# Attention probabilities turned by VectorE and 13 DMAs in place of TensorE, the value product one batch late, GpSimd scaling 13 of 16 batches

## What is computed

```python
scores = jnp.einsum('bhqd,bhkd->bhqk', q, k) / jnp.sqrt(jnp.asarray(HD, x.dtype))
scores = scores + causal_bias
attn = jax.nn.softmax(scores, axis=-1)
out = jnp.einsum('bhqk,bhkd->bhqd', attn, v)
out = out.transpose(0, 2, 1, 3).reshape(b, s, NH * HD)
return out @ wo
```

## Time and profile before

| what | value |
|---|---|
| median of 3 runs | 1897.14 us (1891.51 to 1898.26) |
| profiled execution, first to last instruction | 1893.5 us |
| TensorE busy | 97% |
| VectorE busy | 68% |
| ScalarE busy | 50% |
| GpSimd busy | 29% |
| DMA traffic | 212.37 MB, mean 112 GB/s |

### The profile page before, as it was taken

How to read it: one execution, slowest core, us unless ns; L and a number is a source line. 1 busy time by engine, 2 the same in 40 slices (tenths; PEclk the granted TensorE clock), 3 DMA queues, 4 the chain that set the end, 5 groups by cost and what they waited for, 6 DMA issues and landing times.

```text
span 1893.5 us, 36659 instructions
## 1 busy us (share of the span) xinstructions
PE 1842.4 (97%) x10612; PEld 1359.5 (72%) x10613; DVE 1281.0 (68%) x3173; ACT 949.9 (50%) x3625; POOL 543.2 (29%) x721
## 2 busy tenths in 40 slices
PE   7999999999999999999999999999999999999995
PEld 5887888766668888756667888766667888866663
DVE  4677778754467888764467888764466888855456
ACT  4647776622226777732225777642224777642221
POOL 4752113430022332540032332531031332520014
PEclk9999999999999999999999999999999999999998
DMA  6423220255653330245663340236663331136666
GB/s 165 130 71 107 101 101 6 85 139 143 154 149 102 116 115 7 85 122 142 145 157 89 118 130 27 85 94 147 145 164 93 128 116 44 43 92 149 147 163 172
DMA packets 255292, 212.37 MB, mean 112 GB/s; under 512 B 145826, under 2 KB 226420, under 8 KB 255028
## 3 DMA queue, kind: packets, MB, share of 16 engines
q1 hardware_dynamic: 240808, 174.74, 33.8%
q0 software_dynamic: 13952, 35.33, 6.3%
q10 hardware_dynamic: 380, 0.38, 0.1%
HBM read 137.32 MB, written 73.05 MB: 111 GB/s over the span
## 4 chain that ended last, share of the span: by engine, by line
PE 71%; DVE 9%; ACT 8%; issue 4%; POOL 4%; DMA 3%; SPq 1%; POOLq 0%; DVEq 0%; ACTq 0%
PE ps L930 24%; PE ps L956 12%; ACT parena L1273 8%; PE ps L816 7%; PE ps L896 6%; PE ps L872 4%; PE ps L846 3%; PE ps L861 3%; PE ps L824 3%; POOL qk L591 2%; DVE rope L1601 2%; PE ps L798 2%; PE ps L924 2%; DVE rmax L1621 2%; DVE rope L1605 2%
## 5 line engine op out<-in xcount | busy, mean ns | idle before, releaser
L930 PE MATMUL ps<-arena,xeT 128*128 x1120 | 509.5, 593 | 0.0
L1273 ACT ACTIVATE parena<-ps,nmax 112x112 f32<-112x112 f32 x1024 | 345.6, 387 | 95.3 <-DVE nmax L1622 95.3
L930 PEld LDWEIGHTS ps<-arena,xeT 128*128 128x128 f32 x1120 | 210.1, 190 | 193.5 <-issue 187.3
L591 POOL TENSOR_TENSOR qk<-qk,rope 128x448 f32<-128x448 f32 x128 | 146.3, 1143 | 548.9 <-DVE rope L1605 548.7
L1322 ACT ACTIVATE parena<-ps,er 128x512 f32<-128x512 f32 x140 | 96.2, 687 | 377.1 <-PE ps L930 377.1
L816 PE MATMUL ps<-xnT,wqk_s 128*128 128x224 f32 x1280 | 273.5, 357 | 0.0
L570 POOL DMA_INDIRECT y_in<-sorted_y,pos x114 | 111.2, 975 | 500.6 <-DMA sorted_y<-tarena 397.0
L1273 ACT ACTIVATION_READ_ACCUMULATOR parena<-ps,nmax 112x1 f32 x1024 | 245.9, 240 | 0.0
L896 PE MATMUL ps<-wo_s,oT 128*112 128x256 f32 x1024 | 237.9, 385 | 1.4 <-issue 1.4
L816 PEld LDWEIGHTS ps<-xnT,wqk_s 128*128 128x128 f32 x1280 | 233.5, 191 | 3.1
L1898 DVE SCALAR_TENSOR_TENSOR parena<-parena,ps 128x512 f32<-128x512 f32 x140 | 96.0, 686 | 181.5 <-ACT parena L1322 181.4
(11 more groups left out here) (207 smaller groups left out, 2785.2 us busy)
## 6 DMA issues: line engine op xcount, KB each, us to landing
sorted_y<-tarena SPq DMA_DIRECT2D x140, 128.0 KB
xe<-sorted_x SPq DMA_DIRECT2D x132, 130.0 KB, 2.5
arena<-in_L_ffn_wg_dram SPq DMA_DIRECT2D x32, 512.0 KB, 3.7
arena<-in_L_ffn_wu_dram SPq DMA_DIRECT2D x32, 512.0 KB, 4.6
arena<-in_L_ffn_wd_dram SPq DMA_DIRECT2D x32, 512.0 KB, 5.6
hid_d<-tarena SPq DMA_DIRECT2D x240, 64.0 KB
tarena<-hid_d SPq DMA_DIRECT2D x60, 256.0 KB, 2.8
hid_d<-parena SPq DMA_DIRECT2D x240, 64.0 KB
```

The lines of the kernel that those rows point to most:

```text
L591: pool.tensor_tensor(q, q, rope[m % 2][:, :], ALU.add).then_inc(g_rope, 1)
L930: last = pe.matmul(ps[:, bank, :], xeT[u][:, k, :], w[:, bass.ds(e * 1024 + k * 512, 512)], start=(k == 0), stop=(k == KD - 1))
L1273: last = act.activation(prob[:, n, :], ps[0:S, bank, h * S:h * S + S], ACT.Exp, bias=nmax[:, b % 2, n:n + 1], scale=SCALE, accum_out=rsum[ ...
```

## The change

- `turn_probs` moves from TensorE to VectorE. The half's exponentials (now stored in four column blocks of 28, each padded to 32) are turned in 32x32 blocks into `turned`, and after both halves SyncE moves the blocks between partitions with 13 DMAs (`regroup`), 28 partitions by 2 KB each, into `probT`; the three blocks above the diagonal are left out. `copy_probs` is gone.
- `weigh(b)` runs at the end of iteration b + 1, waits for those DMAs, and is cut into 384 and 64 columns per unit. Output projection, rows' sum, turn and logits follow one batch later than before, the logits two.
- The scaling is done by GpSimd (`scale_probs`, in place) for b below 13, and by VectorE for the last three batches. VectorE's second small instruction of `maxima` is gone (the scores come out negated and scaled, so a minimum does).
- VectorE's order in a batch is new: both maxima first, rotations (three in an even batch, two in an odd one) between them and the reciprocals, then `rows_in`, logits, sums, and the two turns. GpSimd scatters the first part's rows all at once at b = 13.
- At the end of the attention stage the products of tiles 0 and 1 stand between the last projections; the second router part has three batches and the last four.

The core of the diff:

```diff
-PARTS = ((0, 9), (9, 13), (13, 16))
+PARTS = ((0, 9), (9, 12), (12, 16))
...
-NEG = -8.0e9
+FAR = 1.0e9
...
+KB, KW = 4, S // 4
+QB = 4
...
+TNP = PB * KB * PAD
+BLOCKS = [(i, j) for i in range(QB) for j in range(KB) if KW * j <= min(PAD * i + PAD, S) - 1]
+SELF_SCALED = 13
...
+            def regroup(l, b):
+                sp.wait_ge(d_turn, l * 32 + 2 * b + 2)
+                sp.wait_ge(p_ot, l * 32 + 2 * b)
+                for i, j in BLOCKS:
+                    sp.dma_start(probT[PAD * j:PAD * j + KW, i, :, :], turned[PAD * i:PAD * i + KW, j, :, :]).then_inc(ld_pt, 16)
...
-                expert_weights(l)
-                if not last:
...
+                for b in range(B - 1):
+                    regroup(l, b)
+                    if b < E:
+                        expert_weights(l, b)
+                    if b == B - 3 and not last:
...
+                regroup(l, B - 1)
...
+            def scale_probs(l, b, p):
+                pool.wait_ge(d_sum, l * 2 * SELF_SCALED + 2 * b + p + 1)
+                heads_p = prob[0:S, :, 8 * p:8 * p + 8, 0:KW]
+                pool.tensor_tensor(heads_p, heads_p, bc(bc(rrec[:, 8 * p:8 * p + 8], 1, [S, KB, 8]), 3, [S, KB, 8, KW]),
+                                   ALU.mult).then_inc(g_norm, 1)
...
+                    if odd and g + 2 < NP:
+                        in_factors(l, g + 2)
+                    if odd and more:
+                        add_rotated(l, g + 1, 3)
+                    if b < SELF_SCALED:
+                        scale_probs(l, b, 0)
+                    if more:
+                        add_rotated(l, g + 1, 4 if odd else 1)
+                    if b < SELF_SCALED:
+                        scale_probs(l, b, 1)
+                    if more and not odd:
+                        add_rotated(l, g + 1, 2)
+                    if b == PARTS[0][1] + 1:
                         out_factors(l, 0)
+                    if b == RANK_STEP + 2:
+                        scatter_first(l, 0, PARTS[0][1])
...
-                def turn_probs(b, unit):
...
-                    for i in range(4):
-                        last = pe.transpose(ps[0:S, 4 + j, i * S:i * S + S], prob[:, p * 8 + j * 4 + i, :], ident[0:S, 0:S])
-                    last.then_inc(p_pt, 1)
...
-                    if b:
+                    pe.wait_ge(ld_pt, (l * B + b + 1) * 16 * len(BLOCKS))
+                    pe.wait_ge(a_v, l * NP + b // 2 + 1)
+                    if 0 < b < B - 1:
                         pe.wait_ge(d_wo, l * B + b)
...
+                    if b == B - 1:
+                        pe.wait_ge(m_xT, l * NT + 2)
+                    for p in range(2):
+                        if p and b:
...
+                        for q0 in (0, 96):
+                            for j in range(2):
+                                unit = 2 * p + j
+                                out = ps[64 * j:64 * j + 64, weigh_bank(b, p), 0:GN].rearrange("d (h q) -> d h q", h=4)
+                                if q0 == 0:
+                                    out = out[:, :, 0:96].rearrange("d h (i q) -> d i h q", i=3)
+                                    moved = probT[:, 0:3, 4 * unit:4 * unit + 4, :]
+                                else:
+                                    out, moved = out[:, :, 96:S], probT[:, 3, 4 * unit:4 * unit + 4, 0:S - 96]
+                                last = pe.matmul(out, v_s[:, b % 4, unit * HD:unit * HD + HD], moved, start=True, stop=True)
+                        last.then_inc(p_ot, 1)
...
+                        pe.wait_ge(a_exp, l * 32 + (2 if b == 1 else 2 * b - 1))
                         scores(l, b, 0)
...
+                    if more and not odd:
+                        pe.wait_ge(a_t1, l * B + 2 * (g + 1) + 2)
+                        heads_of(l, g + 1, 0, 4)
+                        pe.wait_ge(a_v, l * NP + g + 1)
+                        heads_of(l, g + 1, 1, 5)
+                    if more and odd:
+                        pe.wait_ge(d_rope, l * 40 + (g + 1) * LOADS + 2)
+                        heads_of(l, g + 1, 3, 5)
+                        pe.wait_ge(d_rope, l * 40 + (g + 1) * LOADS + 3)
+                        heads_of(l, g + 1, 4, 4)
...
+                    if b > 2:
+                        pe.wait_ge(a_ot, l * 32 + 2 * b - 3)
+                        route_logits(b - 3)
+                    if b > 1:
+                        out_project(b - 2, 0)
+                        out_project(b - 2, 1)
+                    if more and not odd:
+                        pe.wait_ge(d_rope, l * 40 + (g + 1) * LOADS + 1)
+                        heads_of(l, g + 1, 2, 4)
+                    if more and odd:
+                        pe.wait_ge(d_rope, l * 40 + (g + 1) * LOADS + 4)
+                        values(l, g + 1, 5)
...
+                    if b > 1:
+                        turn_x(b - 2)
                     if odd and g + 2 < NP:
...
-                        pe.wait_ge(a_pt, l * 64 + b * 4 + 3)
+                        pe.wait_ge(d_rope, l * 40 + (g + 1) * LOADS + 5)
...
+                    if b == 1:
+                        pe.wait_ge(moe_done, l + 1)
+                    if b:
+                        weigh(b - 1)
+                    if b == RANK_STEP or b == MID_STEP:
+                        pe.wait_ge(a_exp, l * 32 + 2 * b + 2)
+                        count_rows(0 if b == RANK_STEP else 1, 3)
...
+                pe.wait_ge(ld_mw, (l + 1) * 16 * 3 * E)
+                pe.wait_ge(d_te, l * 2 + 1)
+                e0, e1 = expert_of(0), expert_of(1)
+                pe.wait_ge(m_xT, l * NT + 2)
+                up(0, 0, e0, wg_s, 0, m_g)
+                up(0, 0, e0, wu_s, 1, m_u)
+                pe.wait_ge(d_rt, l * NPART + 2)
+                up(1, 1, e1, wg_s, 2, m_g)
+                pe.wait_ge(a_ot, l * 32 + 2 * B - 3)
+                route_logits(B - 3)
+                for p in range(2):
+                    out_project(B - 2, p)
+                weigh(B - 1)
                 turn_hidden(0)
+                up(1, 1, e1, wu_s, 3, m_u)
+                turn_x(B - 2)
+                pe.wait_ge(a_ot, l * 32 + 2 * B - 1)
+                turn_tile(2, 0, 2)
+                route_logits(B - 2)
...
-                def copy_probs(b, unit):
-                    act.wait_ge(p_pt, l * 64 + b * 4 + unit + 1)
-                    act.activation(probT[:, unit, :], ps[0:S, 4 + unit % 2, 0:GN], ACT.Copy).then_inc(a_pt, 1)
...
-                step(dve.tensor_reduce(rmax[:, hs].rearrange("p (n h) -> p n h", n=2), heads(b, p), AX_X, ALU.max))
-                dve.tensor_scalar(nmax[:, b % 2, hs], rmax[:, hs], -SCALE, None, ALU.mult).then_inc(d_max, 1)
+                dve.tensor_reduce(nmax[:, b % 2, hs].rearrange("p (n h) -> p n h", n=2), heads(b, p), AX_X, ALU.min).then_inc(d_max, 1)
...
+                def sums(b, p):
                     dve.wait_ge(a_exp, l * 32 + 2 * b + p + 1)
                     hs = slice(8 * p, 8 * p + 8)
-                    step(dve.reciprocal(rrec[:, hs], rsum[:, b % 2, hs]))
-                    dve.tensor_tensor(prob[:, hs, :], prob[:, hs, :], bc(rrec[:, hs], 2, [S, 8, S]),
-                                      ALU.mult).then_inc(d_norm, 1)
+                    if b < SELF_SCALED:
+                        if b:
+                            dve.wait_ge(g_norm, l * 2 * SELF_SCALED + 2 * b + p - 1)
+                        dve.reciprocal(rrec[:, hs], rsum[:, b % 2, hs]).then_inc(d_sum, 1)
+                    else:
+                        step(dve.reciprocal(rrec[:, hs], rsum[:, b % 2, hs]))
+                        step(dve.tensor_tensor(prob[0:S, :, hs, 0:KW], prob[0:S, :, hs, 0:KW],
+                                               bc(bc(rrec[:, hs], 1, [S, KB, 8]), 3, [S, KB, 8, KW]), ALU.mult))
+                def turn_probs(b, p):
+                    if b < SELF_SCALED:
+                        dve.wait_ge(g_norm, l * 2 * SELF_SCALED + 2 * b + p + 1)
+                    if b:
+                        dve.wait_ge(ld_pt, (l * B + b) * 16 * len(BLOCKS))
...
+                    hs = slice(8 * p, 8 * p + 8)
+                    dve.transpose(turned[:, :, hs, :].rearrange("k j n q -> k j (n q)"),
+                                  prob[:, :, hs, :].rearrange("q j n k -> q j (n k)")).then_inc(d_turn, 1)
...
+                    if more:
+                        rotate(step, l, g + 1, 3 if odd else 0, 5 if odd else 4)
+                    sums(b, 0)
+                    if more:
+                        rotate(step, l, g + 1, 4 if odd else 1, 4 if odd else 5)
+                    if b >= SELF_SCALED:
+                        turn_probs(b, 0)
+                    sums(b, 1)
+                    if l and b + LEAD < B:
+                        rows_in(step, l, b + LEAD)
+                    if b > 2:
+                        take_logits(b - 3)
+                    if b > 1:
+                        add_attention(b - 2)
+                    if b > 2:
+                        top_two(b - 3)
```

(14 more changed lines are left out.)

383 lines of the change are left out of this document (155 added, 228 removed).

## The result

The changed kernel takes **2138.49 us** (median of 4 runs, 2133.80 to 2145.17) where the kernel before takes 1895.2: a ratio of **1.1287** (95% interval 1.1261 to 1.1313), 13% slower. The prediction was 2012, range 1870 to 2070: the sign is right, the size is not. The profiled execution went from 1893.5 to 2138.6 us, +245 where the sum had +119 with its 3.6 for the median, or +115 span against span.

A forecast was written before the change was run, and what follows sets the result against it. It took TensorE, 97% busy, as the bound before, and port waits between VectorE and GpSimd after. +38.5 us in each of three layers, 0 in layer 0, gave 1893.5 + 115 = 2008, plus 3.6: 2012 us, range 1870 to 2070.

The forecast's parts named there:

- the sign: Whole kernel: the change makes it slower, given a chance of 0.79.
- the sum: Whole kernel: +38.5 us in each layer after the first, 0 in layer 0; +115 in all.
- the forecast's own largest term: Batches 2 to 10, layers 1 to 3: 17.0 us a batch against 14.6, 9 x 2.4 = +22 a layer.
- The waits for the ports: VectorE and GpSimd, both with two SBUF operands, each wait for the other's whole instruction; GpSimd's scalings take 2.07 us.
- the walk: Step-by-step schedule of a pair of batches, layers 1 to 3 up to batch 10: 34.0 us a pair.
- TensorE's clock falls: Rival, chance 0.16: TensorE idles and drops to half clock, each second batch adding 1.5 us x 30: 2055 us.
- there are over 12 us: hidden, unless a DMA's issue exceeds 0.8 us: VectorE's second turn to the value product: `regroup`, say 8 us, fits in over 12 us and costs nothing.
- The DMAs set the pace: Rival, chance 0.04: turn, `regroup`, next turn bound all layers; 15 + 1.3 us a batch at 1 us an issue, 2000 to 2050.
- the 13.4 forecast for layer 0: Batches without `rows_in` (layer 0, and above batch 10): 26.8 us a pair, 13.4 a batch, 1.2 faster.
- batches 14 and 15 ... 46.4, +7.5: Batch 14's scores to tile 2: 13 us for each batch, then 20 us of products; 46.4 against 38.9, +7.5.
- The expert stage keeps its order: Expert stage, behind the attention stage: order unchanged, no term in the sum.
- 3 x 13.4 + 6 = 46.5: Batches 11 to 13: three batches of 13.4 us plus 6 of router's work on VectorE; against 44.5, +2 a layer.

The follow-up runs named there:

- E10: Changed kernel with GpSimd's scalings shrunk to 8 elements a row, timing only: batches 2 to 10 of layer 1 take 15.59 us each.
- E13: Changed kernel with TensorE multiplying unread constants before the router's turn (4 products, 8 in batches 13 and 14): 15.64 us a batch instead of 16.94.
- E1: Changed kernel with one of 13 regrouping DMAs issued, timing only: layer 0 falls from 15.22 to 12.87 us a batch; batches 2 to 10 elsewhere 16.98.
- E6: Changed kernel with `rows_in` moved behind the attention's sum: 15.93 us a batch instead of 16.94, 23 us less in all.
- E4: Changed kernel with each regrouping DMA moving 32 partitions instead of 28: layer 0 from 15.22 to 13.36 us a batch, other layers' batches 2 to 10 17.22.
- E7: Changed kernel with VectorE's first turn behind the attention's sum in all batches, batches 13 to 15 included: 24 us less.
- E9: Changed kernel with 32 partitions a DMA, and `rows_in` and the first turn behind the attention's sum in all batches: 1990 us.
- E11: Changed kernel with GpSimd's scalings shrunk to 8 elements a row and one of 13 regrouping DMAs issued, timing only: 1926 us.
- E5: The changed kernel again, unaltered, as base on the chip of the later runs: 2136.6 us.
- E3: Changed kernel with VectorE scaling all batches itself and one of 13 regrouping DMAs issued, timing only: 18.6 us a batch instead of 16.94.

## Why the prediction missed

**Right.** The sign, and the size of the forecast's own largest term: batches 2 to 10 of layers 1 to 3, 16.94 us a batch against 17.0 forecast. The largest measured loss is another one, from batch 14 on. The waits for the ports are real (22.5 us of VectorE's time in nine batches, E10), the turn takes 1.24 us (forecast 1.25, from 0.71 and 1.43), a batch without both costs takes 13.39 and in layer 0 12.85 us (forecast 13.3 and 13.4). The turns were never held up: of the 128, the longest takes 1.25 us, also the six that overlap a scaling, one of them for 1.06 us. So the forecast had taken it from the Trainium skill (SBUF — State Buffer, "SBUF: two separate sides"), which lists only instructions with two inputs from SBUF or in a two-port mode.

**The 17.0 came out by two errors against each other.** By the walk it is 14.0 and 15.35 us from the scores to VectorE's clamp in an even and an odd batch; in layers 1 and 3 it is 13.0 and 13.1. VectorE's waits for the scalings come to 2.5 us a batch (E10), where the walk has 3.75 (34.0 less 26.5 a pair): of four scalings in a pair one takes 1.69 us and two 1.88, only the fourth 2.1, where the walk has 2.07 for each, and `rows_in`'s second instruction slips in ahead of one. On the other side the walk has 2.1 and 2.65 us from the clamp to the next scores, at full clock; they are 3.7 and 4.2, because the value product runs at 1.2 GHz. Together 34.0 us a pair measured, and 34.1 by the walk, which the prediction has as 34.0. E13 shows the second half: with the clock up, a batch takes 15.64. So the agreement to 0.1 us is luck. The forecast's waits and its rival *TensorE's clock falls* were both at work; the rival had the right mechanism and 1.5 us for it, but in each second batch only, where it came in nearly every one, and it was added to a walk that was already too long.

**The step that failed first: "there are over 12 us: hidden, unless a DMA's issue exceeds 0.8 us".** Two things are wrong in it. The issue was taken from stores at 0.46 us and is 0.79, so a set takes 10.4 us to issue and 1.5 to land, 11.9 instead of 8. That alone is still within the 0.8 us of the condition; in batches 2 to 10 of layers 1 to 3, where a batch takes 17 us, the set is in fact hidden (E1). And the slack was counted from VectorE's turn to the value product a batch later, as if a set were free to take all of that time and a batch were always that long. With one `tarena` and one `probT` the next turn waits for the set and the next set for the product: a loop with a period of its own, 11.9 us plus 2.4 to 4.1. I had this loop as the rival *The DMAs set the pace*, at 0.04, and priced it at 15 + 1.3 for an issue of 1 us; by that rule it gives 13.6 at 0.79, already above the 13.4 forecast for layer 0. It costs 2.4 us a batch in layer 0 and 5 us at the start of every layer (E1), about 40 us in all, without the ends, and it is the floor that E6 and E10 fall onto. E1 and E4 show the loop by fewer and shorter issues; a second buffer of either tile was not tried.

**The term mis-sized most: "batches 14 and 15 ... 46.4, +7.5".** It measured 61.4, +22.5 in layer 1, and the whole stretch to the next layer +24 to +32: 84 of the 129 us that the forecast misses. Of these, 23 us lie behind tile 2, a term that was put at nothing with "The expert stage keeps its order"; what makes them up was not tried. Up to tile 2, the 13 us for a batch took no wait for the DMAs, although the order shows the first turn ahead of the attention's sum there, and every DMA of a moved step was to be counted on its queue: the tile's load stands behind 13 issues. Of TensorE's 20.8 idle us from batch 14 of layer 1 to the next layer (before 3.4), 8.7 end with the clamp behind that turn and 6.3 with the load. E7 gives back 6.8 us a layer, E9 10.9, E11 12.6 of 27.5. The rest, some 15 us a layer, no edit here took away. What the trace shows of it: TensorE's busy time from batch 14 on is 6.6 us longer. One more batch's projection and product (3.7 and 3.25, the latter at half clock) lie behind batch 14's scores and two batches' transposes (3.1) are gone, which is 3.9 of it. The cause of the rest stays open.

**Batches 11 to 13, "3 x 13.4 + 6 = 46.5"** (the sum is 46.2). Measured 54.3, and the excess is all in batch 13: 22.4 to 23.5 us in every run without products of constants, E11 included, and 19.7 to 24.5 in those with them. The rows above say why: routing work ahead of and behind the maxima, then VectorE's own two scalings and a turn, all ahead of the clamp on which TensorE waits. I took 6 us as work beside a period, where it lies in the loop. This is read from the trace; no run moved that work.

**The sum of what the runs support.** From E5 to E11: the DMAs and GpSimd's scalings, with what TensorE's clock loses to the waits for them, together cost 211 us of the 242, and neither alone gives more than a part: E10 (scaling) 40 us, E1 (DMAs) some 80, an estimate with 11 us a layer set off for its chip. To add single effects to a forecast undercounts such a pair.

**Against the kernel before** nothing here is faster. The best version that leaves nothing out is E9, 1990 us, 5.0% slower.

## What to carry to other kernels

Where a step goes through a DMA and back, write down the loop that its buffers close (issue of all its DMAs, landing, the next writer, the next reader) and its period, before asking whether the transfer is hidden; and take the price of an issue from a DMA of the same shape. A bound is such a loop, often through two engines: what counts is what stands between its waits, so moving an instruction out of it (E6, E7) may be worth more than making it shorter, and two loops of nearly equal length hide each other's price until both are cut. When an engine that was 97% busy is left to wait, price its work behind the wait at the lower clock.

## What the runs showed of the hardware

- An issue of 28 partitions by 2 KB from SBUF to SBUF on SyncE takes 0.745 us and most come every 0.79; of 32 partitions every 0.63 (E4); the expert weights' 512 KB from DRAM take 0.42 to 0.58.
- With waits of TensorE of 2.3 us a batch its granted clock stood at half for 302 us of the changed kernel (before 23 us); with 1.9 us of products of constants ahead of each turn for 165 (E13).
- A two-port clamp of 0.29 us took 1.67 us beside a scaling of 1.88, in all 27 steady batches, and ended 0.15 us behind it; the one turn in 32x32 blocks that lay wholly inside a scaling (E9) took 1.245, as alone.
- On the chip of E1 to E4 TensorE's output projection came with gaps of up to 2.2 us in batch 14 of layer 1 in E4 (its weight loads 2.6), and VectorE stood idle for 9 and 12 us ahead of its two maxima, while GpSimd scattered rows. The other layers and E1 to E3 show gaps of the same kind:

```profile
857.52 0.26 PEld L944 LDWEIGHTS ps<-wo_s,oT 128*112 128x112 f32 x1 [2.55 <-issue]
858.95 0.58 PE L944 MATMUL ps<-wo_s,oT 128*112 128x256 f32 x1 [2.23 <-issue]
...
866.19 1.09 DVE L1657 TENSOR_REDUCE nmax<-ps 112x8 f32<-112x896 f32 x1 [12.00 <-remote]
```

These are rows of E4. No trace from the other chips shows such gaps, the changed kernel's own included, and the kernel before took 35 us more on this one; why was not tried.
